# Statistics loads in four buffers, a new order of the first loads, two rows of x ahead, and part of a variance aggregate moved, in a two-layer gated attention kernel

## The chip, the cores and the metric

One core of a Trainium2 chip. The metric is the time of one execution on the device in microseconds, taken several times; the profile is one more execution, recorded by the hardware profiler.

## The reference

x has 128 rows of 256 tokens of 256 channels. Each of two layers normalises x with a group norm (32 groups of 8 channels, mean and variance over all rows and tokens), runs gated attention of 8 heads along each row, and adds the result to x. The second layer also has a key mask.

```python
def _gn(v, G=32, eps=1e-5):
    B_, H_, W_, C_ = v.shape
    g = v.reshape(B_, H_, W_, G, C_ // G)
    m = jnp.mean(g, axis=(1, 2, 4), keepdims=True)
    s = jnp.var(g, axis=(1, 2, 4), keepdims=True)
    return ((g - m) / jnp.sqrt(s + eps)).reshape(v.shape)
# one layer (layer 1 adds mask_bias to the logits)
q, k, v = proj(Wq) * scaling, proj(Wk), proj(Wv)
logits = einsum('abhqc,abhkc->abhqk', q, k) + nonbatched_bias[:, None]
wavg = einsum('abhqk,abhkc->abhqc', softmax(logits), v)
out = einsum('able,oe->ablo', sigmoid(in_data @ Wg.T + gating_bias) * wavg, Wo) + bo
x = x + out
```

The statistics of a group norm need all of x. So layer 0 can start on a row only when the whole of x has been read once, and layer 1 only when layer 0 has finished its last row.

## The kernel before

x lies in memory with the channel outermost: 256 channels (2 times 128 partitions) by 32,768 tokens. The program has four stages in time: a preamble, layer 0, a turn between the layers, and layer 1.

**Preamble.** SP issues the small constants, the weights (eight of 256 KB into w_stage, which lies in probs, and two into x_norm), and then the statistics loads: 16 loads of 2 MB into two buffers x_stat (one in probs, one in bias_k). VectorE first makes the low halves of the weights (L554, L559), then runs bn_stats on 512 tokens at a time, 8 for each load (L569), and releases the buffer through `stat_used`. Behind its statistics stand the mask's arithmetic (L575 to L583), two bn_aggr over 64 chunks (L593), and the short chain that turns them into rstd and shift_x: two tiny matmuls (L829, L831), five small vector instructions, and the square root on ScalarE (L540), between two table loads. On SP the masks' loads, the mask pieces' way out and the loads of bias_q and bias_k (2 MB each, L291 and L298) follow the statistics loads; bias_k waits for the last use of its buffer.

**Layers.** Every engine walks through the same slots (slots, L90 and on), -2 to 132 for each layer, and works in slot s on the rows that its stage of the pipeline has reached: rows s-1, s-2 and s-3 for the logits on VectorE (L618, L631), row s-4 for the gated average, row s-5 for the output. Slots 8 to 123 are a hardware loop. All waits are semaphores, and each engine runs its instructions in the order in which the slot writes them. ScalarE loads row s+2 of x (L456), so that the loads of rows 0 and 1 stand in slots -2 and -1, behind the square root. The normalised row x_norm (L486) needs x_in, rstd and shift_x.

**Drain and turn.** In layer 0 VectorE takes bn_stats of every finished row (L687, slot s for row s-5), and the turn needs the last of them: slots 128 to 132 only finish rows 124 to 127. Then follow two bn_aggr over 128 chunks and the same chain to x_norm. In the drain the last row goes through logits (L631), exponentials (ACT L431, L434), the key sums (POOL L407), the average (PE L739, L746), gated (POOL L380), its halves (L527, L361), the output (PE L766), attn (ACT L495) and y (POOL L374). POOL does these for each row in one fixed order: gated_lo, key sum 0, y, gated of the row before, key sum 1.

Of the kernel before, what the change touches and what calls it, by code (L numbers as in the profile page):

```python
# [34 lines left out]
P = 128  # L35
# [13 lines left out]
GN_EPS = 1e-5  # L49
STAT_TOK = 2048  # L50
STAT_LOADS = ROWS * TOK // STAT_TOK
EXP_LAG = 4
UNROLL = 4
# [60 lines left out]
def build(nc, a, out):  # L114
# [10 lines left out]
    with ctx:  # L125
        def sb(name, shape, dt):
            return ctx.enter_context(nc.sbuf_tensor(name, shape, dt))

        def sem(name):
            return ctx.enter_context(nc.semaphore(name))  # L130
# [17 lines left out]
        stats = sb("stats", [P, CT, ROWS, 6], f32)  # L148
        mean_var = sb("mean_var", [P, CT, 2], f32)
        centred = sb("centred", [P, CT], f32)  # L150
        spread = sb("spread", [P, CT], f32)
# [33 lines left out]
        w_out_stage = x_norm  # L185
        x_stat = [t.rearrange("p h t k -> p (h t k)").rearrange("p (c t) -> p c t", c=CT)
                  for t in (probs[:, 1], bias_k[:, :, :, :])]

# [15 lines left out]
        stack_init, mask_out = sem("stack_init"), sem("mask_out")  # L204
        stat_in = [sem(f"stat_in{i}") for i in range(2)]
        stat_used, w_hi_ready, w_lo_ready = sem("stat_used"), sem("w_hi_ready"), sem("w_lo_ready")
        zeroed, mask_fine_ready, gate_bias_ready = sem("zeroed"), sem("mask_fine_ready"), sem("gate_bias_ready")
        mask_step = sem("mask_step")
        norm_v, norm_c, norm_avg, norm_std = sem("norm_v"), sem("norm_c"), sem("norm_avg"), sem("norm_std")
        x_loaded = [sem(f"x_loaded{i}") for i in range(2)]  # L210
# [45 lines left out]
        def _(sp):  # L256

            sp.dma_start(group_avg[:, :], a["group_avg"]).then_inc(const_in, 16)
            sp.dma_start(ident[:, :], a["ident"]).then_inc(const_in, 16)
            for i, n in enumerate(("L0_conv_gating_bias", "L1_conv_gating_bias")):  # L260
                sp.dma_start(gate_bias[:, i, :], a[n]).then_inc(const_in, 16)
            for i, n in enumerate(("L0_conv_bo", "L1_conv_b_o")):
                sp.dma_start(out_bias[:, i, :], a[n]).then_inc(const_in, 16)
            for l in range(2):
                for m in range(4):
                    sp.dma_start(w_stage[:, l, m], a["w_proj"][l, m].rearrange("(c p) e -> p c e", p=P)
                                 ).then_inc(w_in, 16)
                sp.dma_start(w_out_stage[:, l], a["w_out"][l].rearrange("(c p) e -> p c e", p=P)).then_inc(w_out_in, 16)

            for i in range(2):  # L270
                sp.dma_start(x_stat[i], channel_major(a["xT"], i * STAT_TOK, STAT_TOK)).then_inc(stat_in[i], 16)
            with sp.Fori(1, STAT_LOADS // 2) as c:
                for i in range(2):
                    wait(sp, stat_used, 2 * c + (i - 1), sp_passed)
                    sp.dma_start(x_stat[i], channel_major(a["xT"], c * (2 * STAT_TOK) + i * STAT_TOK, STAT_TOK)
                                 ).then_inc(stat_in[i], 16)
            sp.dma_start(mask_row[:, :], a["mask"]).then_inc(mask_in, 16)
            sp.dma_start(mask_bias[:, :, :], a["mask_k"]).then_inc(mask_in, 16)
            sp.wait_ge(zeroed, 3)
            for i in range(4):  # L280
                sp.dma_start(stack[1][MASK_ROW:MASK_ROW + 4, i], a["k_rows"]).then_inc(stack_init, 16)
            sp.wait_ge(mask_step, 3)
            sp.dma_start(mask_dram.rearrange("b r t -> b (r t)"), mask_pc[:, :, :].rearrange("p r t -> p (r t)")
# [16 lines left out]
            def slot(s):  # L300
# [26 lines left out]
                if isinstance(s.turns, int):  # L327


                    if l == 0 and s.off == -1:  # L330
                        load_bias_q(0)
                        load_bias_k(0)
                    if l == 0 and s.off == ROWS + 1:
                        load_bias_q(1)
                    if l == 0 and s.off == ROWS + 2:
                        load_bias_k(1)
# [77 lines left out]
        def _(act):  # L414
# [32 lines left out]
            def slot(s):  # L447
# [4 lines left out]
                r = s.plus(2)  # L452
                if r.active():
                    i = r.ring(2)
                    wait(act, x_norm_ready, r.plus(-2).count(1, 1), act_passed)
                    act.dma_start(x_in[:, i], channel_major(src[l], r.index() * TOK, TOK)).then_inc(x_loaded[i], 16)  # L456
# [79 lines left out]

            for l in range(2):
                act.wait_ge(norm_avg, 2 * l + 2)
                act.wait_ge(norm_v, 6 * l + 4)
                act.activation(std[:, :], spread[:, :], ACT.Sqrt).then_inc(norm_std, 1)  # L540
                act.preload_act_table_set("exp_and_others")
                if l:
                    for i in range(2):
                        act.wait_ge(y_out[i], 16 * (ROWS // 2 - 2))
                slots(act, l, slot)
# [3 lines left out]
        def _(dve):  # L549

            for l in range(2):
                for m in range(4):
                    dve.wait_ge(w_hi_ready, 4 * l + m + 1)
                    dve.scalar_tensor_tensor(out=w_lo[l][m][:, :, :], in0=w_stage[:, l, m], scalar=W_SCALE,  # L554
                                             in1=w_hi[l][m][:, :, :], op0=ALU.mult, op1=ALU.subtract
                                             ).then_inc(w_lo_ready, 1)
            for l in range(2):
# [3 lines left out]
                                         ).then_inc(w_lo_ready, 1)  # L561

            n = STAT_TOK // 512
            with dve.Fori(0, STAT_LOADS // 2) as c:
                for i in range(2):
                    dve.wait_ge(stat_in[i], c * 16 + 16)
                    for ct in range(CT):
                        for t in range(n):
                            op = dve.bn_stats(stats[:, ct, bass.ds(c * (2 * n) + (i * n + t), 1), :],  # L569
                                              x_stat[i][:, ct, t * 512:(t + 1) * 512])  # L570
                    op.then_inc(stat_used, 1)

# [10 lines left out]
            dve.tensor_scalar(mask_pc[:, 1, :], mask_row[:, :], 1.0 / FINE, None, ALU.mult).then_inc(mask_step, 1)  # L583

            def normalisation(l):

                chunks = ROWS if l else ROWS * TOK // 512
                if l:
                    dve.wait_ge(stats_ready, ROWS)
                else:  # L590
                    dve.wait_ge(stat_used, STAT_LOADS)
                for c in range(CT):
                    op = dve.bn_aggr(mean_var[:, c, :], stats[:, c, 0:chunks, :].rearrange("p a b -> p (a b)"))  # L593
                op.then_inc(norm_v, 1)
# [67 lines left out]
            def slot(s):  # L662
                l = s.layer
                for step in range(8):
                    if s.plus(-1).active():
# [216 lines left out]
```

## Time and profile before

| | |
|---|---|
| time, median of 3 runs | 3749.67 us (3744.16 to 3749.84) |
| the profiled execution's own time | 3750.91 us |
| its span | 3749.0 us |
| mean granted TensorE clock | 0.991 |
| busy: PE / VectorE / ScalarE / POOL | 93% / 94% / 73% / 81% |
| first instruction of layer 0 (x_norm) | at 134.0 us |
| last statistics of layer 0, first x_norm of layer 1 | at 1947.55 and 1960.62 us |

Times inside the profile are microseconds from the start of the span. A row of the timeline gives start, length and instruction, and in brackets how long the engine stood idle before it and what it waited for. Where several alike follow one another they are one row, with their count.

### The profile page before, as it was taken

What the parts mean: (1) busy time and instruction counts of PE and PEld (TensorE: products, weight loads), DVE (VectorE), ACT (ScalarE), POOL (GpSimd) and SP (SyncE); (2) the same over time, 40 slices, a digit from 0 to 9 for tenths busy, and PEclk for the clock granted to TensorE, in tenths of its full rate; (3) what the DMA queues carried; (4) which work ended last, traced back from release to release, by engine and by line L of the source; (5) the groups of instructions that cost most, each with busy time, mean ns of one, the idle gap of its engine ahead of it and who ended that gap; (6) DMA issues with size and microseconds to landing.
All of it is one profiled execution on the core that took longest, in us unless ns stands there. A gap on an engine that the chain in (4) does not pass through costs nothing.

```text
span 3749.0 us, 121609 instructions
## 1 busy us (share of the span) xinstructions
PE 3495.1 (93%) x36360; PEld 2630.4 (70%) x36360; DVE 3539.6 (94%) x11937; ACT 2742.8 (73%) x4625; POOL 3021.8 (81%) x2056
## 2 busy tenths in 40 slices
PE   0499999999999999999968999999999999999997
PEld 0377777777777777777746777777777777777775
DVE  6599999999999999999968999999999999999997
ACT  0377777777777777777746777777787777777775
POOL 1288888888888888888856888888888888888887
PEclk9999999999999999999979999999999999999998
DMA  8555555555555555555534555555555555555553
GB/s 321 173 112 118 113 112 114 115 115 113 115 113 117 113 113 112 118 113 112 114 107 107 119 118 116 120 117 118 120 119 117 117 118 117 119 116 119 120 118 75
DMA packets 450644, 454.08 MB, mean 121 GB/s; under 512 B 42880, under 2 KB 445440, under 8 KB 445968
## 3 DMA queue, kind: packets, MB, share of 16 engines
q1 hardware_dynamic: 241680, 251.85, 35.5%
q10 hardware_dynamic: 208896, 201.38, 19.5%
q8 instruction: 37, 0.61, 0.1%
q14 instruction: 31, 0.25, 0.0%
HBM read 182.39 MB, written 67.24 MB: 67 GB/s over the span
## 4 chain that ended last, share of the span: by engine, by line
PE 58%; DVE 25%; issue 11%; DMA 3%; DVEq 1%; POOL 1%; SPq 1%; ACT 0%; POOLq 0%; ACTq 0%
PE proj_b L712 15%; DVE max_bank L618 10%; PE proj_a L712 9%; PE proj_a L766 9%; PE max_bank L723 8%; PE av_bank L739 7%; PE exp_bank L728 7%; DVE probs L631 6%; PE den_bank L746 3%; DVE row_max L618 3%; DVE stats L687 2%; DMA bias_k<-in_xT 1%; DVE recip L658 1%; DVE fine L637 1%; PE proj_b L757 1%
## 5 line engine op out<-in xcount | busy, mean ns | idle before, releaser
L618 DVE CUSTOM_DVE_ANT_0 max_bank<-max_bank,bias_q 128x256 f32<-128x256 f32 x4096 | 1637.6, 441 | 127.7 <-PE max_bank L723 95.7
L407 POOL TENSOR_TENSOR probs_sum<-probs 128x1024 f32<-128x1024 f32 x512 | 1207.8, 2359 | 308.3 <-ACT probs L434 154.3
L631 DVE TENSOR_TENSOR probs<-exp_bank,bias_k 128x512 f32<-128x512 f32 x2048 | 1390.0, 679 | 7.4 <-PE exp_bank L728 7.4
L723 PE MATMUL max_bank<-k_stack,q_stack 96*128 96x256 f16 (+1 forms) x4096 | 788.5, 274 | 11.8 <-DMA k_stack<-k_lo 9.9
L728 PE MATMUL exp_bank<-q_stack,k_stack 100*128 100x256 f16 x4096 | 784.4, 272 | 8.8 <-DVE probs L631 6.5
L431 ACT ACTIVATE probs<-probs,mask_bias 128x1024 f32<-128x1024 f32 x512 | 573.0, 1149 | 61.4 <-DVE probs L631 61.3
L434 ACT ACTIVATE probs<-probs 128x1024 f32<-128x1024 f32 x512 | 525.7, 1056 | 91.9 <-DVE probs L631 91.8
L618 DVE DVE_READ_ACCUMULATOR2_ANT row_max<- 128x1 f32 x4096 | 568.0, 139 | 0.0
L739 PE MATMUL av_bank<-probs,v_sb 128*32 128x256 f32 x8192 | 550.1, 386 | 3.0 <-ACT probs L431 1.6
L723 PEld LDWEIGHTS max_bank<-k_stack,q_stack 96*128 96x128 f16 (+1 forms) x4096 | 381.5, 98 | 164.0 <-DVE row_max L618 103.5
L728 PEld LDWEIGHTS exp_bank<-q_stack,k_stack 100*128 100x128 f16 x4096 | 395.1, 97 | 71.9 <-DVE probs L631 12.4
L392 POOL TENSOR_TENSOR x_lo<-x_norm,x_hi 128x512 f16<-128x512 f32 x256 | 299.0, 1168 | 147.0 <-ACT x_hi L516 147.0
L380 POOL TENSOR_TENSOR gated<-avg,recip 128x512 f32<-128x512 f32 x256 | 327.9, 1281 | 110.1 <-DVE recip L658 81.7
L374 POOL TENSOR_TENSOR y<-y,attn 128x512 f32<-128x512 f32 x256 | 327.1, 1278 | 101.1 <-ACT attn L495 65.3
L531 ACT ACTIVATE v_sb<-proj_a 128x512 f32<-128x512 f32 x256 | 152.9, 597 | 289.8 <-PE proj_a L712 289.8
L739 PEld LDWEIGHTS av_bank<-probs,v_sb 128*32 128x32 f32 x8192 | 214.0, 109 | 200.5 <-issue 57.6
L444 ACT ACTIVATE k_hi<-proj_b 128x512 f16<-128x512 f32 x256 | 152.8, 597 | 245.6 <-PE proj_b L712 245.6
L746 PE MATMUL den_bank<-probs_sum,ones 128*32 128x256 f32 x4096 | 317.7, 382 | 5.3 <-POOL probs_sum L407 5.3
L400 POOL TENSOR_TENSOR k_lo<-k_f,k_hi 128x512 f16<-128x512 f32 x256 | 296.9, 1160 | 29.5 <-issue 18.1
L400 POOL TENSOR_TENSOR q_lo<-q_f,q_hi 128x512 f16<-128x512 f32 x256 | 296.5, 1158 | 26.2 <-ACT q_f L445 26.2
L361 POOL TENSOR_TENSOR gated_lo<-gated,gated_hi 128x512 f16<-128x512 f32 x256 | 297.8, 1163 | 1.6 <-ACT gated_hi L527 1.6
L486 ACT ACTIVATE x_norm<-x_in,shift_x,rstd 128x256 f32<-128x256 f32 x512 | 278.5, 599 | 7.0 <-DMA x_in<-in_xT 6.8
(120 smaller groups left out, 6919.1 us busy)
## 6 DMA issues: line engine op xcount, KB each, us to landing
q_stack<-q_hi SPq DMA_DIRECT2D x512, 128.0 KB
k_stack<-k_hi SPq DMA_DIRECT2D x512, 128.0 KB
x_in<-in_xT ACTq DMA_DIRECT2D x128, 256.0 KB, 2.7
q_stack<-q_lo SPq DMA_DIRECT2D x256, 128.0 KB
k_stack<-k_lo SPq DMA_DIRECT2D x256, 128.0 KB
y<-in_xT ACTq DMA_DIRECT2D x128, 256.0 KB, 3.0
layer_out<-y ACTq DMA_DIRECT2D x128, 256.0 KB, 2.7
x_in<-layer_out ACTq DMA_DIRECT2D x128, 256.0 KB, 2.7
```

Of the source, the lines that this page charges most:

```text
L400: pool.tensor_tensor(qk_lo[m][:, b], qk_f32[m][:, b], qk_hi[m][:, b], ALU.subtract).then_inc(qk_lo_ready[m], 1)
L407: pool.tensor_tensor(probs_sum[:, g], pr[:, :, 0, :], pr[:, :, 1, :], ALU.add).then_inc(sum_ready, 1)
L431: act.activation(pr, pr, ACT.Exp, bias=mask_bias[:, bass.ds(r.index(), 1), t]).then_inc(probs_ready, 1)
L434: act.activation(pr, pr, ACT.Exp).then_inc(probs_ready, 1)
L618: op = dve.tensor_tensor_reduce(out=max_bank[h % 2][:, t, :], in0=max_bank[h % 2][:, t, :], in1=bias_q[:, h, t, :], scale=1.0 / FINE, scal ...
L631: dve.tensor_tensor(probs[:, r.ring(2), h], exp_bank[h % 2][:, :, :], bias_k[:, h], ALU.add).then_inc(logits_ready, 1)
L712: op = pe.matmul(ps[:, tile, :], lhs, rhs, start=(n == 0), stop=(n == len(terms) - 1))
L723: op = pe.matmul(bank_[:, t, :], q[0:n, t * P:(t + 1) * P], k[0:n, :], start=True, stop=True)
L728: op = pe.matmul(bank_[:, t, :], k[0:n, t * P:(t + 1) * P], q[0:n, :], start=True, stop=True)
L739: op = pe.matmul(av_bank[HC * j:HC * (j + 1), g, :], v_sb[:, r.ring(4), t, HC * h:HC * (h + 1)], probs[:, r.ring(2), h, t, :], start=(t == ...
L746: op = pe.matmul(den_bank[HC * j:HC * (j + 1), g, :], ones[:, :], probs_sum[:, g, j, :], start=True, stop=True)
L766: op = pe.matmul(pa[:, o, :], w[l][:, e, o * P:(o + 1) * P], g[:, b, e, :], start=(n == 0), stop=(n == len(terms) - 1))
```

## The change

1. The 16 loads of 2 MB become 32 of 1 MB, in four buffers (each old buffer is halved). `stat_used` is counted for each, and the loop on SP and on VectorE takes four of them in a turn.
2. SP issues the first four statistics loads before everything else; behind them the weights, the masks, the constants, the four k_rows loads (which wait for POOL's memsets) and rows 0 and 1 of x for layer 0, and only then the loop of the other 28 statistics loads. VectorE does the statistics of the first four buffers, the low halves of the weights and the mask's arithmetic ahead of its loop.
3. For layer 1, SP issues the loads of rows 0 and 1 in slot 128 of layer 0. ScalarE loads only rows 2 and on, in both layers.
4. ScalarE loads the square root's table ahead of the waits for the statistics instead of behind them.
5. At the start of slot 130 of layer 0 VectorE aggregates the first 120 chunks, and writes the result over chunk 119 as if it were one chunk of 120 rows. The final aggregate of layer 1 then runs over 9 chunks instead of 128.

```diff
-STAT_TOK = 2048
+STAT_TOK = 1024
 STAT_LOADS = ROWS * TOK // STAT_TOK
+STAT_BUFS = 4
+EARLY_ROWS = 120
...
         def _(sp):
 
+            for i in range(STAT_BUFS):
+                sp.dma_start(x_stat[i], channel_major(a["xT"], i * STAT_TOK, STAT_TOK)).then_inc(stat_in[i], 16)
+            for l in range(2):
+                for m in range(4):
+                    sp.dma_start(w_stage[:, l, m], a["w_proj"][l, m].rearrange("(c p) e -> p c e", p=P)
+                                 ).then_inc(w_in, 16)
+                sp.dma_start(w_out_stage[:, l], a["w_out"][l].rearrange("(c p) e -> p c e", p=P)).then_inc(w_out_in, 16)
+            sp.dma_start(mask_row[:, :], a["mask"]).then_inc(mask_in, 16)
+            sp.dma_start(mask_bias[:, :, :], a["mask_k"]).then_inc(mask_in, 16)
             sp.dma_start(group_avg[:, :], a["group_avg"]).then_inc(const_in, 16)
             sp.dma_start(ident[:, :], a["ident"]).then_inc(const_in, 16)
...
-            for i in range(2):
-                sp.dma_start(x_stat[i], channel_major(a["xT"], i * STAT_TOK, STAT_TOK)).then_inc(stat_in[i], 16)
-            with sp.Fori(1, STAT_LOADS // 2) as c:
-                for i in range(2):
-                    wait(sp, stat_used, 2 * c + (i - 1), sp_passed)
...
             sp.wait_ge(zeroed, 3)
             for i in range(4):
                 sp.dma_start(stack[1][MASK_ROW:MASK_ROW + 4, i], a["k_rows"]).then_inc(stack_init, 16)
+            for i in range(2):
+                sp.dma_start(x_in[:, i], channel_major(a["xT"], i * TOK, TOK)).then_inc(x_loaded[i], 16)
+            with sp.Fori(1, STAT_LOADS // STAT_BUFS) as c:
+                for i in range(STAT_BUFS):
+                    wait(sp, stat_used, STAT_BUFS * c + (i + 1 - STAT_BUFS), sp_passed)
+                    sp.dma_start(x_stat[i], channel_major(a["xT"], c * (STAT_BUFS * STAT_TOK) + i * STAT_TOK, STAT_TOK)
+                                 ).then_inc(stat_in[i], 16)
             sp.wait_ge(mask_step, 3)
...
+                    if l == 0 and s.off == ROWS:
+                        sp.wait_ge(x_norm_ready, ROWS)
+                        for i in range(2):
+                            sp.wait_ge(y_out[i], 16 * (ROWS // 2 - 4))
+                            sp.dma_start(x_in[:, i], channel_major(x1, i * TOK, TOK)).then_inc(x_loaded[i], 16)
...
                 r = s.plus(2)
-                if r.active():
+                if r.active() and s.active():
...
             for l in range(2):
+                act.preload_act_table_set("sqrt_and_others")
                 act.wait_ge(norm_avg, 2 * l + 2)
...
+            n = STAT_TOK // 512
+
+            def statistics(c):
+                for i in range(STAT_BUFS):
+                    dve.wait_ge(stat_in[i], c * 16 + 16)
+                    for ct in range(CT):
+                        for t in range(n):
+                            op = dve.bn_stats(stats[:, ct, bass.ds(c * (STAT_BUFS * n) + (i * n + t), 1), :],
+                                              x_stat[i][:, ct, t * 512:(t + 1) * 512])
+                    op.then_inc(stat_used, 1)
+
+            statistics(0)
...
+            with dve.Fori(1, STAT_LOADS // STAT_BUFS) as c:
+                statistics(c)
+
+            def early_rows():
+                half = EARLY_ROWS * TOK / 2
+                for c in range(CT):
+                    op = dve.bn_aggr(early_mean_var[:, c, :], stats[:, c, 0:EARLY_ROWS, :].rearrange("p a b -> p (a b)"))
+                op.then_inc(early_stats, 1)
+                dve.wait_ge(early_stats, 1)
+                kept = stats[:, :, EARLY_ROWS - 1, :].rearrange("p c (i m) -> p c i m", i=2)
+                for i in range(2):
+                    dve.memset(kept[:, :, i, 0], half)
+                    dve.tensor_copy(kept[:, :, i, 1], early_mean_var[:, :, 0])
+                    op = dve.tensor_scalar(kept[:, :, i, 2], early_mean_var[:, :, 1], half, None, ALU.mult)
+                op.then_inc(early_stats, 1)
...
-                chunks = ROWS if l else ROWS * TOK // 512
+                first, chunks = (EARLY_ROWS - 1, ROWS) if l else (0, ROWS * TOK // 512)
...
+                if l == 0 and isinstance(s.turns, int) and s.off == EARLY_ROWS + 10:
+                    dve.wait_ge(stats_ready, EARLY_ROWS)
+                    early_rows()
```

The first place at which the order differs is the start of SP's program. Before (x_norm takes the output weights, probs the others and half of the statistics loads):

```order
L258 DMA group_avg<-in_group_avg 128x128
L259 DMA ident<-in_ident 128x128
...
L266 DMA probs<-in_w_proj 128x2x256 x4
L268 DMA x_norm<-in_w_out 128x2x256
L271 DMA probs<-in_xT 128x2x2048
L271 DMA bias_k<-in_xT 128x2x2048
...
L275 DMA probs<-in_xT 128x2x2048
L275 DMA bias_k<-in_xT 128x2x2048
...
L277 DMA mask_row<-in_mask 128x256
```

In the changed kernel:

```order
L263 DMA probs<-in_xT 128x2x1024 x2
L263 DMA bias_k<-in_xT 128x2x1024 x2
L266 DMA probs<-in_w_proj 128x2x256 x4
L268 DMA x_norm<-in_w_out 128x2x256
...
L270 DMA mask_bias<-in_mask_k 128x256
L271 DMA group_avg<-in_group_avg 128x128
...
L281 DMA x_in<-in_xT 128x2x256 x2
...
L285 DMA bias_k<-in_xT 128x2x1024
```

Four statistics loads have moved ahead of the weights, and the others stand behind the weights, the masks, the constants and two rows of x.

The second place is VectorE in the drain of layer 0, at the end of slot 129 and in slot 130 (the logits of row 127 are the rows probs<-exp_bank). Before:

```order
L631 TENSOR_TENSOR probs<-exp_bank,bias_k 128x512
L687 BN_STATS stats<-y 128x6
L631 TENSOR_TENSOR probs<-exp_bank,bias_k 128x512 x3
L644 SCALAR_TENSOR_TENSOR avg<-gate_tanh,av_bank 128x512
L649 STREAM_TRANSPOSE den_turned<-den_bank 128x512
L631 TENSOR_TENSOR probs<-exp_bank,bias_k 128x512
```

In the changed kernel:

```order
L661 TENSOR_TENSOR probs<-exp_bank,bias_k 128x512
L720 BN_STATS stats<-y 128x6
L604 BN_AGGR early_mean_var<-stats 128x2 x2
L609 MEMSET stats 128x2
L610 COPY stats<-early_mean_var 128x2
L611 TENSOR_SCALAR stats<-early_mean_var 128x2
L609 MEMSET stats 128x2
L610 COPY stats<-early_mean_var 128x2
L611 TENSOR_SCALAR stats<-early_mean_var 128x2
L661 TENSOR_TENSOR probs<-exp_bank,bias_k 128x512 x3
L674 SCALAR_TENSOR_TENSOR avg<-gate_tanh,av_bank 128x512
```

The early aggregate stands ahead of the last four logits instructions of row 127.

## Rows read from the trace of the kernel before

**Rows 1.** The page: span, busy time of each engine.

```profile
span 3749.0 us, 121609 instructions
PE 3495.1 (93%) x36360; PEld 2630.4 (70%) x36360; DVE 3539.6 (94%) x11937; ACT 2742.8 (73%) x4625; POOL 3021.8 (81%) x2056
```

**Rows 2.** Timeline, start of the preamble: start us, length us, instruction.

```profile
0.76 0.43 SPq L258 DMA_DIRECT2D group_avg<-in_group_avg  x1
...
7.92 6.92 POOL L349 MEMSET k_stack<- 32x8192 f16 x1
...
13.13 0.63 ACT L418 ACTIVATE w_hi0q<-probs 128x512 f16<-128x512 f32 x1 [11.08 <-DMA probs<-in_w_proj]
...
13.79 0.69 DVE L554 SCALAR_TENSOR_TENSOR w_lo0q<-probs,w_hi0q 128x512 f16<-128x512 f32 x1 [13.79 <-ACT w_hi0q L418]
...
19.82 4.83 DVE L569 BATCH_NORM_STATS2 stats<-probs 128x512 f32 x8
```

**Rows 3.** The waits of VectorE, 20 to 118 us.

```profile
DVE stats L569 <- DMA probs<-in_xT: 16.4, 7, 2.9
```

**Rows 4.** Timeline, one statistics load of 2 MB, issue and use.

```profile
42.79 0.37 SPq L275 DMA_DIRECT2D bias_k<-in_xT  x1
...
50.20 4.85 DVE L569 BATCH_NORM_STATS2 stats<-bias_k 128x512 f32 x8 [0.52 <-DMA bias_k<-in_xT]
```

**Rows 5.** Busy time by stretch; the last three columns: PEclk, DMA share, GB/s.

```profile
45.00:49.00 4.00, 0.00 (x0) 0.00 (x0) 4.00 (x7) 0.00 (x0) 0.00 (x0) 1.00 1.00 424
...
9.50:12.50 3.00, 0.00 (x0) 0.00 (x0) 0.00 (x0) 0.00 (x0) 3.00 (x1) 1.00 1.02 325
...
32.30:106.90 74.60, 0.00 (x0) 0.00 (x0) 58.17 (x97) 0.00 (x0) 0.00 (x0) 1.00 0.87 335
```

**Rows 6.** The page, DMA issues: count, KB each, us to landing.

```profile
x_in<-in_xT ACTq DMA_DIRECT2D x128, 256.0 KB, 2.7
```

**Rows 7.** Timeline, last statistics to the first x_norm.

```profile
112.31 4.84 DVE L569 BATCH_NORM_STATS2 stats<-bias_k 128x512 f32 x8 [0.59 <-DMA bias_k<-in_xT]
...
118.57 3.63 DVE L593 BATCH_NORM_AGGREGATE mean_var<-stats 128x2 f32<-128x384 f32 x2
...
124.41 1.28 ACT L540 ACT_TABLE_LOAD   x1 [105.97 <-DVE spread L603]
124.49 0.95 ACTq L456 DMA_DIRECT2D x_in<-in_xT  x2
...
125.70 0.20 ACT L540 ACTIVATE std<-spread 128x2 f32<-128x2 f32 x1
...
134.00 1.09 ACT L486 ACTIVATE x_norm<-x_in,shift_x,rstd 128x256 f32<-128x256 f32 x2 [6.79 <-DMA x_in<-in_xT]
```

**Rows 8.** Timeline, VectorE in slot 130, logits of row 127.

```profile
1922.65 0.67 DVE L631 TENSOR_TENSOR probs<-exp_bank,bias_k 128x512 f32<-128x512 f32 x1
1924.66 1.29 DVE L631 TENSOR_TENSOR probs<-exp_bank,bias_k 128x512 f32<-128x512 f32 x2 [1.33 <-PE exp_bank L728]
...
1927.09 0.65 DVE L631 TENSOR_TENSOR probs<-exp_bank,bias_k 128x512 f32<-128x512 f32 x1
```

**Rows 9.** Timeline, POOL in slot 130.

```profile
1928.12 1.27 POOL L374 TENSOR_TENSOR y<-y,attn 128x512 f32<-128x512 f32 x1 [1.09 <-ACT attn L495]
...
1930.59 2.35 POOL L407 TENSOR_TENSOR probs_sum<-probs 128x1024 f32<-128x1024 f32 x1
```

**Rows 10.** Timeline, TensorE, two of the 12 matmuls of output rows 125 and 126.

```profile
1925.63 0.38 PE L766 MATMUL proj_a<-gated_hi,w_out_hi 128*128 128x256 f16 x2
...
1934.58 0.63 PE L766 MATMUL proj_a<-gated_hi,w_out_lo 128*128 128x256 f16 x2
```

**Rows 11.** Timeline, last row's statistics, the aggregate of layer 1.

```profile
1947.55 0.75 DVE L687 BATCH_NORM_STATS2 stats<-y 128x6 f32<-128x256 f32 x2 [7.56 <-POOL y L374]
1948.34 7.10 DVE L593 BATCH_NORM_AGGREGATE mean_var<-stats 128x2 f32<-128x768 f32 x2
```

**Rows 12.** Timeline, ScalarE, the first x_norm of layer 1.

```profile
1960.62 1.09 ACT L486 ACTIVATE x_norm<-x_in,shift_x,rstd 128x256 f32<-128x256 f32 x2 [0.23 <-DMA x_in<-layer_out]
```

More of the change, by code:

```diff
@@ L149, in build @@
         mean_var = sb("mean_var", [P, CT, 2], f32)
+        early_mean_var = sb("early_mean_var", [P, CT, 2], f32)
         centred = sb("centred", [P, CT], f32)
@@ L185, in build @@
         w_out_stage = x_norm
-        x_stat = [t.rearrange("p h t k -> p (h t k)").rearrange("p (c t) -> p c t", c=CT)
-                  for t in (probs[:, 1], bias_k[:, :, :, :])]
+        x_stat = [t.rearrange("p h t k -> p (h t k)").rearrange("p (i c t) -> p i c t", i=2, c=CT)[:, i]
+                  for t in (probs[:, 1], bias_k[:, :, :, :]) for i in range(2)]
         def bank(name):
@@ L204, in build @@
         stack_init, mask_out = sem("stack_init"), sem("mask_out")
-        stat_in = [sem(f"stat_in{i}") for i in range(2)]
+        stat_in = [sem(f"stat_in{i}") for i in range(STAT_BUFS)]
         stat_used, w_hi_ready, w_lo_ready = sem("stat_used"), sem("w_hi_ready"), sem("w_lo_ready")
@@ L208, in build @@
         mask_step = sem("mask_step")
+        early_stats = sem("early_stats")
         norm_v, norm_c, norm_avg, norm_std = sem("norm_v"), sem("norm_c"), sem("norm_avg"), sem("norm_std")
@@ L263, in _ @@
                 sp.dma_start(out_bias[:, i, :], a[n]).then_inc(const_in, 16)
[L264 to L268, printed above, removed]
-            for i in range(2):
-                sp.dma_start(x_stat[i], channel_major(a["xT"], i * STAT_TOK, STAT_TOK)).then_inc(stat_in[i], 16)
-            with sp.Fori(1, STAT_LOADS // 2) as c:
-                for i in range(2):
-                    wait(sp, stat_used, 2 * c + (i - 1), sp_passed)
[L275 to L278, printed above, removed]
             sp.wait_ge(zeroed, 3)
@@ L561, in _ @@
                                          ).then_inc(w_lo_ready, 1)
[L563 to L571, printed above, removed]
             dve.wait_ge(mask_in, 32)
@@ L583, in _ @@
             dve.tensor_scalar(mask_pc[:, 1, :], mask_row[:, :], 1.0 / FINE, None, ALU.mult).then_inc(mask_step, 1)
+            with dve.Fori(1, STAT_LOADS // STAT_BUFS) as c:
[12 more added lines that the diff above has]
+                op.then_inc(early_stats, 1)
             def normalisation(l):
-                chunks = ROWS if l else ROWS * TOK // 512
+                first, chunks = (EARLY_ROWS - 1, ROWS) if l else (0, ROWS * TOK // 512)
                 if l:
                     dve.wait_ge(stats_ready, ROWS)
+                    dve.wait_ge(early_stats, 2)
                 else:
@@ L592, in normalisation @@
                 for c in range(CT):
-                    op = dve.bn_aggr(mean_var[:, c, :], stats[:, c, 0:chunks, :].rearrange("p a b -> p (a b)"))
+                    op = dve.bn_aggr(mean_var[:, c, :], stats[:, c, first:chunks, :].rearrange("p a b -> p (a b)"))
                 op.then_inc(norm_v, 1)
```

## The prediction

> **What bounds the kernel now.** I read the page first: VectorE is busy for 94% of the span and TensorE for 93% [rows 1]. So the two layers are bound by those two engines, and the change touches neither in its steady slots. What it can move lies where they are idle: the preamble, up to x_norm at 134.00 us [rows 7], and the turn between the layers, from the last statistics at 1947.55 to x_norm at 1960.62 [rows 11, 12]. The timeline, the waits and the busy time by stretch were read for those two. In the preamble the reader is to see VectorE waiting for a load in every turn: 16.4 us in 7 waits for the buffer in probs [rows 3], where a load issued at 42.79 is used at 50.20 [rows 4]. The transfers run at 424 GB/s while one is moving, but at 335 GB/s over the whole stretch, with the queues busy for 0.87 of it [rows 5]: a 2 MB load is issued only when its buffer is free, and with two buffers the queue runs dry for some 2 us of each turn.
>
> **Part 1: the loads and the statistics.** Removed is that gap. A load of 1 MB is 1.0486 million bytes, at 424 GB/s 2.47 us. The statistics of one are half of a row of eight instructions, 4.84 / 2 = 2.42 us [rows 7]. After releasing a buffer there are three others to work on, 3 x 2.42 = 7.3 us, and a new load needs some 2.1 us of latency (2.7 us for 256 KB [rows 6], less 0.6 us of moving) and 2.5 us of moving, 4.6 together. The queue no longer runs dry.
>
> The clock of the preamble, step by step. SP issues the first load at 0.76 [rows 2], so it lands at 0.76 + 2.1 + 2.47 = 5.3; the fourth at 5.3 + 3 x 2.47 = 12.7. Behind them come the ten weight loads, 2.62 million bytes, at the 325 GB/s that the same transfers show [rows 5]: 8.1 us, to 20.8, the last of the eight for w_hi by 20.0. Masks and constants (0.4 million bytes) take 1.2 us, and two rows of x 1.6 us: the queue comes to the fifth statistics load at 23.6. SP must have issued it by then. It waits for the memset that ends at 14.84 [rows 2], then has ten issues of up to 0.5 us, so it is there by 20.
>
> VectorE: the first four buffers are done at 12.7 + 2.42 = 15.1, then it idles until w_hi exists at 20.0 + 0.66 (13.79 less 13.13 [rows 2]) = 20.7. The ten low halves took 19.82 - 13.79 = 6.03 us [rows 2], the mask's arithmetic 118.57 - 117.15 = 1.42 us (the last statistics end at 112.31 + 4.84 [rows 7]). So its loop starts at 28.1, and 28 x 2.42 = 67.8 us more give **95.9**. The transfers alone give 23.6 + 28 x 2.47 + 2.42 = 95.2. The two are level; I take 96.0 for the start of the aggregate, against 118.57 [rows 7]: **-22.6 us**. The bounds: nothing under 94, since VectorE's own work, 77.4 + 6.0 + 1.4, and the two idle times of about 10 us cannot be had away; above, if 1 MB transfers with rows half as long moved midway between 424 and 325 GB/s [rows 5], at 375: 2.80 us each, 23.6 + 78.4 + 2.4 = 104.4.
>
> The Trainium skill (DMA: Bandwidth & Descriptors, Specifications) puts a core's reading from HBM at about 358 GB/s, and SBUF — State Buffer tells the author to estimate by that. By it a load would take 2.93 us, the last statistics would end at 108, and the gain of this part would be an estimated 10.6 us. The row of 424 GB/s over four microseconds speaks against it here.
>
> **Part 2: rows of x ahead, and the table.** Before, 15.43 us pass from the aggregate's start to x_norm (134.00 - 118.57 [rows 7]), and the last 6.79 of them are a wait for x_in, which was issued at 124.49 behind 4 MB of biases [rows 7]. Now x_in has long landed. What is left: the aggregate 3.63, the chain to the square root 124.41 - 122.20 = 2.2, the root 0.20, the exponential's table 1.3, 0.1 of issue: 7.4 us. **-8.0 us**. The square root's table, 1.28 us [rows 7], is loaded while ScalarE has nothing to do. The biases now overlap only work that comes before their use: bias_q is needed some 16 us after x_norm, and both are in by about 107.
>
> At the turn the same two save less: from the aggregate's end (1948.34 + 7.10 = 1955.44) to x_norm at 1960.62 are 5.18 us [rows 11, 12], now 2.2 + 0.20 + 1.3 + 0.1 = 3.8: **-1.4 us**. The loads in slot 128 on SP cost 1 us of issue ahead of nothing that is waited for.
>
> **Part 3: the early aggregate.** From 384 elements (3.63 us for both halves [rows 7]) and 768 (7.10 [rows 11]) an aggregate costs 0.16 us and 9.04 ns an element for the pair. 9 chunks are 54 elements: 0.65 us, so **-6.45 us** at the turn. The early one, 720 elements, is 6.67 us, and with a wait and six tiny instructions 7.4 us. This is not hidden. In the order it stands ahead of the last four logits of row 127, and in slot 130 VectorE idles just once, 1.33 us ahead of the second of them [rows 8]. Those logits feed everything that follows. Counting on: the block runs from 1922.65 to 1930.05; logits 4, 5 and 6 end at 1931.85, average and transpose (0.6 each) at 1933.1, logits 7 at 1933.7, where before it was 1927.74 [rows 8]: 6.0 us later. TensorE stands behind logits 5 for its own exp_bank matmul and then does the output of row 125, 1.4 us at the shape of 1925.63, but 2.7 us at that of 1934.58, as it runs after a pause [rows 10]. Then attn, y, gated and the key sum of row 127 follow on POOL, which before stood at 1928.12 and 1930.59 [rows 9]: the key sum comes 6.1 us late with a fast TensorE, 7.5 with a slow one. From there to 1947.55 the chain is unchanged. I take **+6.5 us**: the two amounts cancel. Bounds: 0, if something I do not see covers it, and 7.5. VectorE's real idle time stands later, 7.56 us ahead of the last statistics [rows 11].
>
> **The sum**, against the profiled execution's own 3750.91 us: -22.6 - 8.0 - 1.4 - 6.45 + 6.5 = -32.0, so 3719.0 us. The profiled execution is 1.2 us above the median of 3749.67; the difference is inside the spread of the three runs and I leave it.
>
> **The rivals.**
> - *The early aggregate is hidden.* VectorE does idle for over 17 us between 1922 and 1949, and if the block fell into that the +6.5 goes: 3712.5 us. Against it stands the order. 0.06.
> - *The stream is at its ceiling already.* If the 335 GB/s of the whole stretch [rows 5] were what the memory gives and not the effect of the gap, a load takes 3.13 us, the statistics end at 23.6 + 87.6 + 2.4 = 113.6, and only 5.0 of the 22.6 us come: 3736.6 us. Against it: 0.87 of busy queues, and the gap in every turn. 0.07, with the slower transfers of part 1 at its near side. The skill's 358 GB/s, named above, would be this rival in milder form, at about 3731 us as an estimate.
> - *Slower.* The loads do not overlap each other: the latency of each comes on top of its moving, as where one 2 MB load takes 7.4 us from issue to use [rows 4]. 1 MB would then take about 5 us, the 28 end at 23.6 + 140 + 2.4 = 166, 47 us later than now, less 9.4 for part 2: some 3789 us. It decides from 3.6 us a load (23.6 + 28 x 3.6 + 2.4 = 127, less 9.4 is level). Against it: the load of rows 4 was issued 2 us before the one ahead of it had landed and did not pay those 2 us twice. 0.02.
> - *The change does little*: the four buffers behave as two, because the loop on SP waits for the buffer just used. It reads as a wait for the oldest, so this is 0.02, at about 3740 us.
>
> **How the numbers follow.** My forecast has 0.83. Its own range, from the bounds of part 1 and the two TensorE speeds, is 3716 to 3728. The range I give, 3712 to 3730, takes in the hidden aggregate and leaves out the ceiling, the slower case and the useless buffers. A run of this kernel can tell 0.2%, 7.5 us, from no change. All but the slower case and a worst form of the ceiling are faster by more: faster 0.97, same 0.01, slower 0.02.
>
> **What would show it.** The aggregate of layer 0 starts near 96, VectorE's waits for statistics loads in the loop shrink to a few tenths of a microsecond or nothing, and the stretch from 30 to 90 moves over 400 GB/s. x_norm follows the aggregate's start by 7.4 us with no wait for a DMA. In the drain the early aggregate is followed by logits without idle time, POOL waits longer for its key sum, the last statistics come about 6.5 us later after the drain's start than now, and the final aggregate takes 0.65 us. I am wrong if VectorE still waits about 1 us a buffer (the ceiling), if x_norm waits for something else, or if the stretch from the last maxima of row 127 to the last statistics has not grown.

## The result, and the profile after

The changed kernel takes 3822.32 us (median of 5 runs, 3818.49 to 3823.80) against 3749.26 us of the kernel before measured beside it: a ratio of 1.0196, 95% interval 1.0182 to 1.0210. It is about 2% slower. The forecast was 3719.0 us with a range of 3712 to 3730.

The page of the changed kernel, where its lines answer to those of [rows 1] and to the time spent by instruction fetches, which the forecast never looked at:

```profile
span 3821.2 us, 121672 instructions
PE 3532.9 (92%) x36360; PEld 2639.1 (69%) x36360; DVE 3541.9 (93%) x11945; ACT 2744.2 (72%) x4625; POOL 3024.8 (79%) x2056
...
PEclk9999999999999999999989999999999999999999
...
q14 instruction: 173, 1.42, 0.1%
```

In the kernel before, the same queue had

```profile
q14 instruction: 31, 0.25, 0.0%
```

VectorE is busy for as long as before (3541.9 us against 3539.6) and executes 8 instructions more that compute. The time is idle time, and the first x_norm of each layer and the last one say where it lies. The timeline of ScalarE after (rows 0 and 127 of layer 0, rows 0 and 127 of layer 1):

```profile
108.83 1.09 ACT L496 ACTIVATE x_norm<-x_in,shift_x,rstd 128x256 f32<-128x256 f32 x2
...
1852.25 1.09 ACT L496 ACTIVATE x_norm<-x_in,shift_x,rstd 128x256 f32<-128x256 f32 x2
...
1931.81 1.09 ACT L496 ACTIVATE x_norm<-x_in,shift_x,rstd 128x256 f32<-128x256 f32 x2
...
3749.01 1.09 ACT L496 ACTIVATE x_norm<-x_in,shift_x,rstd 128x256 f32<-128x256 f32 x2
```

Before, the first and the third stood at 134.00 and 1960.62 [rows 7, 12], the second and the fourth at

```profile
1877.81 1.09 ACT L486 ACTIVATE x_norm<-x_in,shift_x,rstd 128x256 f32<-128x256 f32 x2
...
3677.15 1.09 ACT L486 ACTIVATE x_norm<-x_in,shift_x,rstd 128x256 f32<-128x256 f32 x2
```

| stretch | before | after | difference |
|---|---|---|---|
| start to the first x_norm | 134.0 | 108.8 | -25.2 |
| layer 0, row 0 to row 127 | 1743.8 | 1743.4 | -0.4 |
| drain and turn | 82.8 | 79.6 | -3.2 |
| layer 1, row 0 to row 127 | 1716.5 | 1817.2 | **+100.7** |
| last x_norm to the end | 71.8 | 72.2 | +0.4 |

So the change gains 28.8 us up to the first x_norm of layer 1 and loses 100.7 us in layer 1, in whose steady slots it changes no instruction. Between rows 8 and 120 a turn of four rows takes 57.96 us there instead of 54.46; in layer 0 it takes 55.40 in both. VectorE's waits in layer 1 of the changed kernel, 20 turns of the loop, name it:

```profile
DVE max_bank L648 <- issue: 56.8, 20, 3.0
DVE max_bank L648 <- PE max_bank L756: 41.0, 82, 1.5
```

Before, there was no row of the first kind, and the second stood at 26.9 us. "issue" means that nothing the profile shows was waited for: no semaphore, no DMA of the program. It comes once a turn. The timeline around one:

```profile
3135.11 0.68 DVE L661 TENSOR_TENSOR probs<-exp_bank,bias_k 128x512 f32<-128x512 f32 x1
3138.57 0.43 DVE L648 CUSTOM_DVE_ANT_0 max_bank<-max_bank,bias_q 128x256 f32<-128x256 f32 x1 [2.77 <-issue]
```

And the DMA queues over the same 20 turns (2140 to 3300 us) hold packets that the kernel before does not have at all there:

```profile
q14 instruction: 100, 0.82, 0.3%
```

These are 8 KB packets of instructions, five for each turn. They stand at the loop's edge: in one turn VectorE's branch is recorded at 2554.10 us, packets start at 2554.7 and 2555.2, and the next maxima start at 2558.08, after 2.98 us of idle time. The other engines wait with it: TensorE is busy for 1109.9 of the 1160 us of this stretch, where before it was for 1153.2. Its granted clock over the stretch is 0.98 of full, before 1.00: in 14 of the 20 turns it falls for a short time to the lower of its two levels (1.2 instead of 2.4 GHz), each time behind such a pause (from 2558.10 to 2562.00 TensorE is busy for 1.6 of 3.9 us, at a mean of 0.85). VectorE's waits for TensorE grow with it, from 26.9 to 41.0 us over the 20 turns, which is 0.7 of the 3.5 us a turn; 2.8 are the idle time put down to issue.

### The profile page after: what moved, and what is told of

Same layout as the page of the kernel before. It is cut to its first block, busy times and chain, and to the rows that moved or that the text cites. A ratio compares the mean times of both kernels' runs of the same rounds, so it can differ in the third digit from the quotient of the medians.

```text
span 3821.2 us, 121672 instructions
## 1 busy us (share of the span) xinstructions
PE 3532.9 (92%) x36360; PEld 2639.1 (69%) x36360; DVE 3541.9 (93%) x11945; ACT 2744.2 (72%) x4625; POOL 3024.8 (79%) x2056
## 4 chain that ended last, share of the span: by engine, by line
PE 51%; DVE 30%; issue 15%; DMA 1%; DVEq 1%; SPq 1%; POOL 1%; ACT 0%; POOLq 0%; ACTq 0%
PE proj_b L745 14%; DVE max_bank L648 12%; PE proj_a L799 9%; DVE probs L661 7%; PE proj_a L745 7%; PE max_bank L756 7%; PE exp_bank L761 6%; PE av_bank L772 5%; DVE row_max L648 4%; PE den_bank L779 2%; DVE stats L720 2%; DVE recip L688 1%; DVE fine L667 1%; DVE stats L569 1%; PE proj_b L790 1%
## 5 line engine op out<-in xcount | busy, mean ns | idle before, releaser
L410 POOL TENSOR_TENSOR k_lo<-k_f,k_hi 128x512 f16<-128x512 f32 x256 | 297.0, 1160 | 118.3 <-ACT k_f L455 95.9
```

The lines of the kernel that those rows point to most:

```text
L410: pool.tensor_tensor(qk_lo[m][:, b], qk_f32[m][:, b], qk_hi[m][:, b], ALU.subtract).then_inc(qk_lo_ready[m], 1)
```

## The experiments

**Theory F** (fetch): a loop on VectorE whose instructions lie across one block boundary too many is fetched anew in each turn; the change moved layer 1's loop there. **Theory D**: the new row loads or DMA contention slow layer 1. **Theory C**: chip or clock. I counted VectorE's records up to the end of each loop's first turn, taking the statistics loop once: the change puts the loop of layer 0 18 instructions later and that of layer 1 29 later (the eleven between them are the early aggregate: the eight that compute and three waits). The tool of the first experiments is a filler that does nothing but take up instruction places:

```diff
+        pad = sb("pad", [P, 28, 2], f32)
...
             statistics(0)
+            for i in range(28):
+                dve.memset(pad[:, i, :], 0.0)
```

### The change with 28 memsets behind the first statistics

> The changed kernel with 28 memsets of a 128x2 tile added on VectorE behind the first four buffers' statistics, where it idles 4.95 us; they move everything behind them on VectorE by 28 instructions and do nothing else. Theory F (fetch): the loop of layer 1 on VectorE lies so that its instructions are fetched again in each turn, which costs 3.49 us a turn of four rows; shifted by 28 it does not, so the time is 3822.3 - 100.7 = about 3722 us, the 2.8 us idle times put down to issue are gone and queue 14 carries fetches only outside the loops. Theory D (the rows of x loaded by SP, or DMA contention in layer 1): nothing changes, about 3822. Theory C (the chip or its clock): about 3822 or scattered.

Measured: 3765.26 us, ratio to before 1.0040 (1.0026 to 1.0054). That is neither number. Layer 1 is as before (1715.5 us from row 0 to row 127, 54.45 us a turn, no packet on queue 14 in its loop), as theory F says and D and C don't. But now layer 0 has the packets, 102 in 20 of its turns,

```profile
q14 instruction: 102, 0.84, 0.2%
```

and takes 1789.4 us instead of 1743.4. The filler had pushed layer 0's loop from +18 to +46. I had not reckoned its place. The price is another one as well: 1.56 us a turn instead of 3.49, and no idle time put down to issue; VectorE's waits name TensorE instead (27.1 us in 21 waits). That the price depends on where in the turn the fetches fall would be the obvious reading, but it is not shown, and the run with 165 memsets speaks against it: in its layer 1 the first packets start 1.0, 3.9 and 6.4 us behind the branch, here at 1.0, 4.2 and 6.7, and it pays 3.4 us a turn. Why this loop is cheaper stays open.

### The kernel before with 29 memsets

```diff
         def _(dve):
 
+            for i in range(29):
+                dve.memset(pad[:, i, :], 0.0)
             for l in range(2):
```

> The kernel before with 29 such memsets at the start of VectorE's program, where it idles 13.8 us; 29 is the shift of the layer 1 loop that the change brought. Theory F: layer 1 takes 100 us more, so about 3850 us, with one idle time of 2.8 us in each of 29 turns; layer 0 as before. Theories D and C: 3749, since nothing of the change's loads is in it.

Measured: 3922.46 us, ratio 1.0467 (1.0449 to 1.0484), 173.7 us slower. Layer 1 takes 1814.1 us, +97.6 as expected; layer 0, which I had expected unchanged, takes 1818.1, +74.3. Both loops have five packets a turn (the whole profile has 312 on queue 14 instead of 31, and 37 on the other instruction queue as before, so queue 14 is VectorE's), and VectorE waits in layer 0 (500 to 1660 us, 20 turns):

```profile
DVE max_bank L621 <- issue: 50.3, 20, 2.7
```

Nothing of the change is in this kernel, only 29 idle-time memsets, and it loses more than twice what the change lost. So the place of the loops alone can cost this much, and theories D and C are not needed for it; that it was the place that cost the change its 100 us is shown by the memsets in the drain, below. TensorE's clock is not needed either: the granted clock of the 20 turns in layer 0 is 1.00, and a turn costs 2.6 us more all the same.

### The change without the early aggregate

```diff
-                if l == 0 and isinstance(s.turns, int) and s.off == EARLY_ROWS + 10:
-                    dve.wait_ge(stats_ready, EARLY_ROWS)
-                    early_rows()
...
-                    dve.wait_ge(early_stats, 2)
...
-                first, chunks = (EARLY_ROWS - 1, ROWS) if l else (0, ROWS * TOK // 512)
+                first, chunks = (0, ROWS) if l else (0, ROWS * TOK // 512)
```

> The changed kernel without the early aggregate: the final one runs over all 128 chunks again. Its layer 1 loop stands 18 instructions later than before instead of 29. Theory F: the cost of layer 1 is there in full (3822) or not at all (3722), by where the boundary lies, nothing between; the drain is 6 to 7.5 us shorter and the last aggregate 6.45 longer, so within 1 us of those two. A theory that the early aggregate itself slows layer 1 (through its values or its waits): 3722. Theory D: 3822.

Measured: 3720.01 us, ratio 0.9923 (0.9906 to 0.9939). With both loops 18 places later there is no fetch in either, layer 1 takes 1714.7 us. So the rest of the change is worth 28.8 us, and the eleven instructions of the early aggregate cost 102.3. By itself this run could not tell F from "the early aggregate slows layer 1"; the memsets in the drain can.

### The kernel before with 165 memsets

The same edit as with 29.

> The kernel before with 165 memsets at the start of VectorE's program (some 7 us, inside the 13.8 us of idle time). Theory F with boundaries every 256 instructions: now the loop of layer 0 lies across one boundary too many, and that of layer 1 does not, so layer 0 takes about 100 us more, layer 1 as before: about 3850 us. Theories D and C: 3749.

Measured: 3919.97 us, in one run. Both loops are slow (57.91 and 57.87 us a turn, 100 and 103 packets in 20 turns), where I had expected only layer 0's. 165 is 37 modulo 128: a boundary every 256 instructions, my assumption, is wrong if each boundary has one slow stretch of places (29 and 165 are slow, 0 and 90 are not, see below), and one every 128 fits.

### The change with 28 memsets in the drain

```diff
+                if l == 0 and isinstance(s.turns, int) and s.off in (ROWS + 3, ROWS + 4):
+                    for k in range(14):
+                        dve.memset(pad[:, 14 * (s.off - ROWS - 3) + k, :], 0.0)
```

> The changed kernel with 28 memsets on VectorE in the drain of layer 0 (14 ahead of slot 131, 14 ahead of slot 132, in idle time): the loop of layer 0 keeps the place that it has in the change, where nothing was fetched again, and that of layer 1 comes to the place where the first experiment had it (57 instructions behind the kernel before), where nothing was fetched either. Theory F: no fetches in either loop, 3822.3 - 101 = about 3721 us, so equal to the run without the early aggregate (3720.0) within 2 us. A theory that the early aggregate costs something of its own in layer 1: over 3725.

Measured: 3720.13 us, ratio 0.9922 (0.9908 to 0.9935). As expected, to 1 us. The whole change stands in this kernel, its work and its row loads, and the 102 us are gone through 28 instructions that do nothing. It also equals the run without the early aggregate: that edit gains nothing by itself. A rival falls with it: the tile that the memsets write moves the tiles behind it in memory. It is the same here and in the first experiment; only the place of the 28 memsets differs, and layer 0 takes 1743.4 us here and took 1789.4 there.

### The same with the aggregate in slot 132

```diff
-                if l == 0 and isinstance(s.turns, int) and s.off == EARLY_ROWS + 10:
+                if l == 0 and isinstance(s.turns, int) and s.off == EARLY_ROWS + 12:
```

> The same with the early aggregate at the start of slot 132 instead of slot 130, where VectorE idles 7.57 us ahead of the last statistics and the aggregate takes 6.98. Theory F with the prediction's part 3: the logits of row 127 come 6 to 7 us earlier and the last statistics are not delayed by more than 0.5 us, so 5.5 to 6.5 us under the run before it, about 3715 us. If the delay in the drain was not due to the aggregate's place: no difference.

Measured: 3711.70 us, ratio 0.9901 (0.9886 to 0.9916), 8.4 us under the run before it and **the fastest of all**, 37 us under the kernel before. VectorE in the drain of this kernel:

```profile
1896.42 0.67 DVE L662 TENSOR_TENSOR probs<-exp_bank,bias_k 128x512 f32<-128x512 f32 x1
1898.43 1.29 DVE L662 TENSOR_TENSOR probs<-exp_bank,bias_k 128x512 f32<-128x512 f32 x2 [1.34 <-PE exp_bank L765]
...
1914.53 3.40 DVE L605 BATCH_NORM_AGGREGATE early_mean_var<-stats 128x2 f32<-128x720 f32 x1
...
1922.13 0.74 DVE L724 BATCH_NORM_STATS2 stats<-y 128x6 f32<-128x256 f32 x2
1922.90 0.66 DVE L624 BATCH_NORM_AGGREGATE mean_var<-stats 128x2 f32<-128x54 f32 x2
```

The logits of row 127 have only their old 1.34 us of idle time, and the aggregate fills the pause ahead of the last statistics almost exactly. From row 127's x_norm to the next layer's first are 75.5 us, against 81.2 in the run before it: 5.7 us, and that is what the aggregate's place is worth. Most of the rest of the 8.4 lies in layer 1 (1712.9 against 1715.8 us), where I have no mechanism for it; layer 1 took between 1712.1 and 1720.5 us in the kernels without fetches.

### The kernel before with 90 memsets

> The kernel before with 90 memsets at VectorE's start. So far shifts of 0, 18 and, for layer 1, 57 were free of fetches, and 29, 46 and 165 (which is 37 modulo 128) had them. Theory F with blocks of 128 instructions (8 KB, the size of the fetches): 90 is past the bad stretch in both loops, no fetches, 3749 us. If it is not the place modulo 128 but any shift beyond some 20 instructions: 3850 to 3920 us.

Measured: 3751.67 us, in one run; no packet of queue 14 in either loop, 55.40 and 54.57 us a turn. It is not "the more instructions, the slower".

### Two buffers of 2 MB in the change

```diff
-STAT_TOK = 1024
+STAT_TOK = 2048
-STAT_BUFS = 4
+STAT_BUFS = 2
```

(on the kernel without the early aggregate; the two buffers are again whole).

> The change without the early aggregate and with the statistics loads as they were, two buffers of 2 MB, everything else as in the change: the value of the four buffers alone. With them the 28 MB behind the first four took 72.2 us on VectorE (29.24 to 101.45). With two buffers the period for 4 MB was 12.35 us, seven of them are 86.5 us: the aggregate starts at about 116 and the time is 14 us above the 3720.0 of the run without the early aggregate, 3734 us. If most of the gain came from the order of the loads and not from the buffers: under 3725.

Measured: 3734.12 us, ratio 0.9961 (0.9946 to 0.9976); expected 3734. The aggregate starts at 116.65 us. Of the 28.8 us the four buffers are worth 14.1.

### The weights first

```diff
-            for i in range(STAT_BUFS):
-                sp.dma_start(x_stat[i], channel_major(a["xT"], i * STAT_TOK, STAT_TOK)).then_inc(stat_in[i], 16)
             for l in range(2):
                 for m in range(4):
...
+            for i in range(STAT_BUFS):
+                sp.dma_start(x_stat[i], channel_major(a["xT"], i * STAT_TOK, STAT_TOK)).then_inc(stat_in[i], 16)
             sp.dma_start(mask_row[:, :], a["mask"]).then_inc(mask_in, 16)
```

> The run without the early aggregate, with the first four statistics loads behind the ten weight loads instead of ahead of them; VectorE's order is unchanged. If the order of the loads is worth what the timeline says: the first statistics start at about 13.5 instead of 5.9, VectorE has no idle time before the weights' low halves, its loop starts at about 32.5 instead of 29.2 and the first x_norm comes 3.3 us later, 3723.3 us. If the stream of loads is the limit and not VectorE: no difference, 3720.0.

Measured: 3718.27 us, ratio 0.9918 (0.9902 to 0.9935), against 3720.01 and 0.9923 of its base, the change without the early aggregate; so no difference. VectorE's first statistics start at 14.81 us instead of 5.92 and its loop at 32.55 instead of 29.24, but the aggregate only 1.2 us later:

```profile
14.81 5.03 DVE L569 BATCH_NORM_STATS2 stats<-probs 128x6 f32<-128x512 f32 x8 [14.81 <-DMA probs<-in_xT]
...
32.55 4.84 DVE L569 BATCH_NORM_STATS2 stats<-probs 128x512 f32 x8
37.32 4.83 DVE L569 BATCH_NORM_STATS2 stats<-bias_k 128x512 f32 x8
...
102.69 3.64 DVE L622 BATCH_NORM_AGGREGATE mean_var<-stats 128x2 f32<-128x384 f32 x2
```

While its buffers are full VectorE takes 4.77 us for two of them (32.55 to 37.32); in the changed kernel it took 5.12 from the start of its loop (29.24 to 34.36), and this one falls to the same pace later. The stream is the limit, and which loads come first matters to it little.

### The rows of x behind the square root

```diff
-            for i in range(2):
-                sp.dma_start(x_in[:, i], channel_major(a["xT"], i * TOK, TOK)).then_inc(x_loaded[i], 16)
...
-                if r.active() and s.active():
+                if r.active() and (s.active() or l == 0):
```

> The run without the early aggregate, with rows 0 and 1 of x for layer 0 loaded by ScalarE behind the square root again (those of layer 1 as in the change). Before, that wait was 6.79 us, behind 4 MB of biases issued just ahead. Now bias_q goes out at 99.2 and bias_k at 101.4, and the rows' loads at about 107.5, so they wait only for what is left of the biases, to about 111.5: x_norm 3 to 4 us later, 3723.5 us. If the whole of the 6.8 us comes back: 3726.8. If the biases are through by then: x_norm 1.5 us later, 3721.5.

Measured: 3722.19 us, ratio 0.9932 (0.9915 to 0.9948), 2.2 us above the same base in time; in the profile the first x_norm stands at 111.28 instead of 109.0, behind a wait:

```profile
111.28 1.09 ACT L494 ACTIVATE x_norm<-x_in,shift_x,rstd 128x256 f32<-128x256 f32 x2 [3.89 <-DMA x_in<-in_xT]
```

So the rows ahead are worth 2 to 3 us here, not the 6.8 of before. By my reading most of that wait belonged to the biases, which now go out earlier; no run moves them alone.

### The kernel before with 22 memsets

> The kernel before with 22 memsets at VectorE's start, to narrow the place of the boundary, which lies above a shift of 18 and at or below 29 for both loops. Theory F: each layer is either as before (54.5 and 55.4 us for four rows) or slow (57.9), nothing between; so 3749, about 3835 or 3920 us. It cannot be told beforehand which.

Measured: 3744.31 us, in one run; no fetches. The boundary lies above 22 and at or below 29 for both loops. All places seen so far, as a shift against the kernel before, with the time of a turn:

| kernel | layer 0 | layer 1 |
|---|---|---|
| before | 0: 55.40 | 0: 54.46 |
| change without the early aggregate | 18: 55.39 | 18: 54.43 |
| before + 22 | 22: 55.39 | 22: 54.44 |
| the change | 18: 55.40 | 29: **57.96** |
| before + 29 | 29: **57.97** | 29: **57.82** |
| before + 165 (37 modulo 128) | 165: **57.91** | 165: **57.87** |
| change + 28 early | 46: **56.96** | 57: 54.45 |
| change + 28 in the drain | 18: 55.39 | 57: 54.43 |
| before + 90 | 90: 55.40 | 90: 54.57 |

## Why the prediction was wrong

**The premise, in its first paragraph**: that the two layers are bound by VectorE and TensorE, and "the change touches neither in its steady slots". That was the step that failed, for 100.7 us. It is true of what the slots do and false of where they stand in VectorE's program. The order showed that VectorE's program grows by a few rows ahead of the loop, and I used it only to see which instruction stands ahead of which. The 31 packets "instruction" on queue 14 stood in the profile of before, and none of them lay inside a loop; that both loops of VectorE were just inside what can be kept, and by how few places, I did not ask. The trace agrees with what the Trainium skill states (Runtime: NRT & Kernel Launch, Instruction fetch mechanics): an engine holds a small window of its program, filled in order, and a taken branch to a place outside it has to fetch before it goes on. The page gives 32 KiB for the window. Five packets of 8 KB a turn, against none where it fits, are in line with a loop body that reaches into a fifth 8 KB block; I have not seen the window's size itself. Two things do not fit smoothly. The page has refills of 16 KiB, 256 instructions, where this queue has packets of 8 KB and the slow places fit a repeat every 128; here the measurement decides. And the trace records only 298 and 285 instructions a turn, which at 128 to a block would reach into four blocks at most, not five: either some take more than one place in the program, or the picture of the window is incomplete. No run tells which.

**No rival held it either.** The slower rival had serialised loads as its mechanism, at 3789 us with 0.02. It was wrong in mechanism; a general allowance for VectorE's program moving was missing.

**Part 1** had its mechanism right and its size short. The aggregate starts at 101.45 us, not 96.0, so 17.1 us earlier than before instead of 22.6. The profile of the changed kernel, busy time by stretch and the waits of VectorE in the loop:

```profile
30.00:90.00 60.00, 0.00 (x0) 0.00 (x0) 57.32 (x94) 0.00 (x0) 0.00 (x0) 1.00 1.03 409
```

```profile
DVE stats L569 <- DMA probs<-in_xT: 1.3, 2, 0.7
```

The queue no longer runs dry, as forecast. But the stream of 1 MB loads runs at 409 GB/s, where I had taken the 424 of a 2 MB load [rows 5]: 2.56 us a load instead of 2.47, over 28 loads 2.5 us. So the transfers set the pace and not VectorE, which the forecast had level with them (95.2 and 95.9 us). From the transfers' 95.2 to the measured 101.45 are 6.2 us: these 2.5, then 3.1 for the term of 1.2 us for masks and constants, which was too small: with it and the two rows of x the loop's first load was to be in at 23.6 + 2.5 = 26.1, and VectorE waited for it until 29.24. The queue was at work all that time, but on small pieces, among them four constants of 1 KB that landed 0.6 to 0.7 us after one another:

```profile
22.40:25.00 2.60, 0.00 (x0) 0.00 (x0) 2.60 (x5) 2.60 (x6) 0.00 (x0) 1.00 1.05 109
```

The remaining 0.7 us are one wait of VectorE, ahead of the statistics at 42.69. SP was later than I had it too, 21.48 instead of 20, but not the limit: the rows of x that it had issued at 20.12 took 5.8 us to land, behind what stood in the queue. What held SP were the weight loads of w_hi, 4.37 and 5.96 us for four each, where I had up to 0.5 us for one:

```profile
3.06 4.37 SPq L266 DMA_DIRECT2D probs<-in_w_proj  x4
...
7.98 5.96 SPq L266 DMA_DIRECT2D probs<-in_w_proj  x4
...
21.48 1.12 SPq L285 DMA_DIRECT2D probs<-in_xT  x2
```

The rule of the Trainium skill that I weighed (DMA: Bandwidth & Descriptors, Specifications), about 358 GB/s for a core, does not hold here: 409 GB/s over 60 us. The same page's figure for a single core's stream of 1 MiB loads with rows of 4 KiB (DMA: Bandwidth & Descriptors, iDMA fabric, its table of load streams), 408.7 GB/s, does hold, and with it part 1 would have come 2.5 us nearer.

**Part 2** held. From the aggregate's start at 101.45 us to x_norm are 7.38 us (to 108.83), forecast 7.4, with no wait for a DMA. How it splits was not as I had it: the run with the rows behind the square root gives 2 to 3 us for having them ahead. At the turn, from the aggregate's end (1927.47 + 0.66) to 1931.81 are 3.68 us, forecast 3.8.

**Part 3** held. The early aggregate and its small instructions take 6.98 us (forecast 7.4), the final one 0.66 (forecast 0.65), and the drain pays for it:

```profile
1895.82 6.65 DVE L604 BATCH_NORM_AGGREGATE early_mean_var<-stats 128x2 f32<-128x720 f32 x2
...
1902.80 2.08 DVE L661 TENSOR_TENSOR probs<-exp_bank,bias_k 128x512 f32<-128x512 f32 x3
...
1926.68 0.75 DVE L720 BATCH_NORM_STATS2 stats<-y 128x6 f32<-128x256 f32 x2 [7.57 <-POOL y L384]
```

From the start of slot 129's last statistics to the last statistics of the layer are 31.2 us (1895.49 to 1926.68) against 25.2 before: 6.0 more, forecast 6.0 to 7.5 with 6.5 taken. The experiments confirm both halves: with the fetches away the early aggregate changes nothing (3720.13 against 3720.01), and in slot 132 it gains.

With the fetches away the whole change gains 28.3 us (3748.42 to 3720.13) where the sum had 32.0. In the profiled executions, 29.2 us apart, the first x_norm comes 25.6 us earlier than before, where the sum had 30.6; the turn gives 1.6 us, where it had 1.4; another 2.0 us are small differences in the layers and at the run's end, for which it had no term and which are inside what layer 1 varies by.

## What to carry to other kernels

When an edit adds or removes instructions on an engine that runs a long hardware loop, first look at the instruction packets of the profile's DMA queues inside that loop, before and after: eleven instructions ahead of a loop cost 6% in it here (54.46 to 57.96 us a turn), and a filler of 28 that do nothing gave it back. A kernel that is measured with and without an edit should be measured with the loop in a place without fetches in both, or the edit is credited with the loop's place. And work that is moved into a drain belongs where its engine waits longest, not at its start: the same aggregate was worth nothing in slot 130, and in slot 132 the drain and turn were 5.7 us shorter.

## What was unexpected of the hardware

Instruction fetches of VectorE's loops cost 1.56 to 3.5 us a turn of some 55 us, with five 8 KB packets a turn in every case. They came at shifts of 29, 46 (layer 0) and 165 instructions, and not at 0, 18, 22, 57 (layer 1) or 90. That fits a repeat every 128 instructions and speaks against one of 256. The pauses can also lower TensorE's granted clock: 0.98 over layer 1 of the changed kernel, 1.00 before. A stream of 1 MB loads kept 409 GB/s over 60 us, at four in flight. Behind four loads of 1 MB still on their way, the issues of eight 256 KB loads held SP for 0.47 to 3.1 us each, 1.3 in the mean, against at most 0.47 in the kernel before; and four constants of 1 KB took some 2.6 us of a queue that was busy throughout.
